# Two attentions of a two-layer network: the last projection of a step is rounded behind the next step's exponentials

## The reference

```python
q = (x @ Wq).reshape(b, n, HEADS, DIM_HEAD)
k = (context @ Wk).reshape(b, m, HEADS, DIM_HEAD)
v = (context @ Wv).reshape(b, m, HEADS, DIM_HEAD)
sim = einsum('bihd,bjhd->bhij', q, k) * SCALE
out = einsum('bhij,bjhd->bihd', softmax(sim), v) @ Wout + bout
```

## Time and profile before

| | us |
|---|---|
| median of 3 runs | 1023.07 |
| lowest, highest run | 1023.05, 1027.87 |
| the profiled execution's own time | 1026.1 |
| its span, first to last instruction | 1024.2 |
| attention A, first to last maximum | 61 to 459 |
| attention C, first exponential to last | 707 to 917 |

### The profile page before, as it was taken

One profiled execution on the slowest core, in us unless ns is written; L12 is line 12 of the kernel. 1 busy time (PEld: TensorE's weight loads), 2 busy tenths in 40 slices (PEclk: granted clock), 3 DMA queues, 4 the chain that ended last, 5 costly groups with the idle time before them and its releaser, 6 DMA issues. The chain is left out here.

```text
span 1024.2 us, 23424 instructions
## 1 busy us (share of the span) xinstructions
PE 824.4 (80%) x8736; PEld 506.2 (49%) x8808; DVE 756.2 (74%) x1541; ACT 709.8 (69%) x1179; POOL 627.7 (61%) x574
## 2 busy tenths in 40 slices
PE   3788799999999999997434999967777869875676
PEld 3534465556555656565122676622444536554243
DVE  3857888778877887775686455548979878876797
ACT  3269799889988999991441444436787877991574
POOL 1059677877787778780455666433686857872443
PEclk9989899999999999996666999989898999996799
DMA  8749999999999999993883988972999998990265
GB/s 212 235 80 159 173 178 185 173 167 180 178 184 170 178 172 168 175 178 62 204 292 70 182 187 181 165 243 47 185 169 192 234 203 134 189 171 16 39 116 134
DMA packets 504878, 167.96 MB, mean 164 GB/s; under 512 B 477728, under 2 KB 495328, under 8 KB 504736
## 3 DMA queue, kind: packets, MB, share of 16 engines
q1 hardware_dynamic: 501024, 156.25, 82.5%
q0 software_dynamic: 3744, 10.23, 3.5%
HBM read 37.04 MB, written 11.14 MB: 47 GB/s over the span
## 5 line engine op out<-in xcount | busy, mean ns | idle before, releaser
L521 POOL TENSOR_TENSOR A_PHL<-A_pr,A_PHL 128x508 f16<-128x508 f32 x256 | 294.0, 1154 | 92.1 <-ACT A_pr L802 91.7
L801 ACT ACTIVATE A_PHL<-A_ps,A_negmax 128x508 f16<-128x508 f32 x256 | 190.1, 743 | 14.5 <-DVE A_negmax L1051 12.8
L802 ACT ACTIVATE A_pr<-A_ps,A_negmax 128x508 f32<-128x508 f32 x256 | 191.8, 749 | 0.0
L521 POOL TENSOR_TENSOR C_PHL<-C_pr,C_PHL 128x512 f16<-128x512 f32 x128 | 149.7, 1177 | 58.0 <-ACT C_pr L802 57.8
L1051 DVE TENSOR_REDUCE A_negmax<-A_ps 128x2 f32<-128x1016 f32 x128 | 154.3, 1206 | 0.0
L647 PE MATMUL A_ps<-A_K,A_Q 64*128 64x512 f16 x768 | 106.5, 383 | 18.0 <-ACT A_pr L802 13.9
L665 PE MATMUL A_ps<-A_VH,A_PT 128*128 128x65 bf16 (+1 forms) x1024 | 108.1, 196 | 7.7 <-DMA A_PT<-A_PHL 7.7
L666 PE MATMUL A_ps<-A_VL,A_PT 128*128 128x64 f16 (+1 forms) x1024 | 108.1, 193 | 0.0
L667 PE MATMUL A_ps<-A_VH,A_PT 128*128 128x65 bf16 (+1 forms) x1024 | 108.0, 194 | 0.0
L665 PEld LDWEIGHTS A_ps<-A_VH,A_PT 128*128 128x128 f16 (+1 forms) x1024 | 94.8, 98 | 22.2 <-DMA A_PT<-A_PHL 10.7
L801 ACT ACTIVATE C_PHL<-C_ps,C_negmax 128x512 f16<-128x512 f32 x128 | 89.6, 700 | 20.2 <-DVE C_negmax L1051 17.8
(11 more groups left out here) (342 smaller groups left out, 2286.4 us busy)
## 6 DMA issues: line engine op xcount, KB each, us to landing
A_PT<-A_PHL SPq DMA_TRANSPOSE x256, 3.4
M_raw<-in_L_ffn_w_in SPq DMA_DIRECT2D x4, 1024.0 KB, 8.1
M_raw<-in_L_ffn_w_out SPq DMA_DIRECT2D x4, 1024.0 KB, 9.2
C_yc<-routed_rows SPq DMA_DIRECT2D x8, 512.0 KB, 5.1
M_rows<-M_xhl SPq DMA_DIRECT2D x4, 512.0 KB, 9.1
out<-X SPq DMA_DIRECT2D x16, 128.0 KB, 2.1
X<-in_x SPq DMA_DIRECT2D x1, 1536.0 KB, 14.0
ct_split<-A_CT SPq DMA_DIRECT2D x4, 384.0 KB, 3.0
```

The source lines that it names most:

```text
L521: pool.tensor_tensor(PHL[:, e % PRING, 1, 0:KEYS], pr[:, e % RING, 0:KEYS], PHL[:, e % PRING, 0, 0:KEYS], ALU.subtract).then_inc(pl_ready. ...
L801: a.activation(PHL[:, e % PRING, 0, 0:KEYS], o, ACT.Exp, bias=nm[:, n % 4, h:h + 1])
L802: a.activation(pr[:, e % RING, 0:KEYS], o, ACT.Exp, bias=nm[:, n % 4, h:h + 1]).then_inc(p_ready.sem, 1)
```

## The change

The jobs of each step are sorted so that q, k and v come last; this also is PE's order now. If the last job of a step is a q, k or v and the next step has fewer than two jobs, that job is late: ACT rounds it one step later, behind the next four exponentials (those of the step in which it was projected) instead of ahead of them, and DVE takes its low part behind the next maximum instead of ahead of it. All other jobs stay. In A 28 query, 25 key and 16 value jobs become late, in C 13 query and 13 key jobs. The sort puts a transpose or an image job ahead of a projection in 18 steps of A.

```diff
+    early, late_of = {}, {}
+    for step in sorted(at):
+        at[step].sort(key=lambda u: u[0] in "qkv")
+        spread = at[step][-1][0] in "qkv" and len(at.get(step + 1, [])) < 2
+        early[step] = at[step][:-1] if spread else at[step]
+        late_of[step] = at[step][-1:] if spread else []
...
             for g in range(G + TAIL):
                 if 1 <= g <= G:
                     weights(g - 1)
-                for u in at.get(g, []):
+                for u in late_of.get(g - 1, []) + early.get(g, []):
                     if u[0] in HI_KINDS:
                         high(u)
...
             for g in range(G + TAIL + 1):
-                for u in at.get(g - 1, []):
+                for u in early.get(g - 1, []):
                     low(u)
                 if g < G:
                     wait(v, s_filled, g + 1)
...
                     nb = g // U + 1
+                for u in late_of.get(g - 1, []):
+                    low(u)
+                if g < G:
                     if ipa and nb < B and g % U in (10, 12, 14):
```

## The result

The changed kernel takes 1055.63 us (median of 3, from 1055.27 to 1058.41) against 1023.07 before: ratio 1.0293, 95% interval 1.0245 to 1.0341. It is 32.6 us slower; 18 were forecast, and the time lies 0.6 us above the range. The profiled execution has a span of 1053.4 us, 29.2 more than that of before.

What follows compares the result with a forecast made beforehand. The prediction took PE to bound attention A. Added latency gave 15.7 us in A and 8.6 in C, 24.3 together, less 6 struck: +18 us, a median of 1041 us, range 1020 to 1055.

Steps and rivals of the forecast that it cites:

- late key, eleven pairs of A: Light key pairs of A shorter than 5.96 us grow to that floor from scores to scores; +4.2 us.
- late value, seven places: In A, value products one step after their projection wait for the late low part, 0.85 us at full cost; +4.6 us.
- normalised rows, steps 24, 56, 88: In A's batches 0 to 2, a late key's low part holds DVE ahead of the normalised rows; 1.5 us each, +4.5.
- layernorm chain, other pairs of steps 0 to 17: In A's batch 0, where DVE bounds, the maximum goes ahead of what PE waits for; 1.2 us twice, +2.4.
- C, six light quads (steps 12, 16, 28, 44, 48, 52): In C, query pairs shrink to 4.6 us, key pairs grow to 6.4; +0.5 per quad, +3.0 us.
- strike of a quarter: Over A and C, 6 us taken off the 24.3 because part falls where PE already waits for exponentials.
- the floor of 5.96: Shortest time in us from scores 4c-2 to scores 4c with a late key, through maximum, exponentials, rounding and low part.
- costs PE nothing by itself: Claim that putting the projection behind a transpose in 18 steps of A adds no PE time; 0 us.
- Works as meant: Rival: ACT's waits for projections in A and C are on the path, half recovered, 1010 us; chance 0.11.
- Cancel: Rival: boundaries find slack and C wins what A loses, 1019 to 1028 us; chance 0.11.
- The clock falls: Rival: every second of 24 new PE holes brings a stretch at the lower clock, +17 us, 1058; chance 0.06.
- what would show the forecast: Signs: some 30 PE waits of 0.7 to 1.1 us for keys; ACT waits for maximum instead; A batches 104 to 106 us.

Runs made afterwards that it cites:

- e7: The changed kernel with ACT rounding every job at its old place, only DVE's low parts late; ratio 1.0174 to the kernel before, A loop 410.4 us.
- e8: The changed kernel with DVE taking low parts at their old place, only ACT's roundings late; ratio 1.1329 to the kernel before, A loop 505.9 us.
- e3: The changed kernel, sorted as there, but only key jobs late; ratio 1.0210 to the kernel before.
- e4: The changed kernel, sorted as there, but only query jobs late; ratio 1.0021 to the kernel before.
- e1: The changed kernel with its sort alone and no job late; ratio 1.0066 to the kernel before.
- e2: The changed kernel with the image turn sorted last, so the values of steps 35, 67 and 99 aren't late; ratio 1.0227 to the kernel before.
- e9: The changed kernel without the sort and with only query jobs late; ratio 0.9972 to the kernel before.
- first and third set: Groups of experiments timed beside the kernel before, which had medians of 1024.8 us (first: e1 to e4) and 1026.5 us (third: e8 and two repeats of e9).

## Why the prediction was right, and where it wasn't

The direction and the mechanism hold: no work was added, latency was, in the loop score, maximum, exponential, rounding, low part, score. e7 and e8 take its two links apart, and e3 and e4 show that the distance to the first use is what counts. The size was too small, +18 for +32.6 us. The sizes of the terms, from the pitches of scores (the time from the scores of one pair of steps to those of the next) in both traces:

| term | forecast | measured |
|---|---|---|
| late key, eleven pairs of A | +4.2 | +6.1 |
| late value, seven places | +4.6 | +4.1 |
| normalised rows, steps 24, 56, 88 | +4.5 | -0.9 |
| layernorm chain, other pairs of steps 0 to 17 | +2.4 | -1.7 |
| image, steps 34, 66, 98 | 0 | +7.3 |
| steps 46 and 78 | 0 | +1.8 |
| pair of step 120, half clock | 0 | +1.7 |
| other pairs with `o` (22, 38, 54, 70, 86) | 0 | +1.4 |
| A (with 0.1 of other pairs) | +15.7 | +19.8 |
| C, six light quads (steps 12, 16, 28, 44, 48, 52) | +3.0 | +2.15 |
| C, all other pairs, the layernorm chains among them | +5.6 | +4.91 |
| C, last step | 0 | -0.62 |
| strike of a quarter | -6 | 0 |

That A came within 4.1 us of its forecast is in part luck. Two terms were 9.5 us too high (normalised rows, layernorm chain), and four that the forecast had at nothing or not at all (image, steps 46 and 78, step 120, `o`) brought 12.2.

**Late keys.** Ten of the eleven pairs sum to +4.7, for which the forecast has 3.9 (from the pitches before, the shortfalls of all eleven sum to 4.4, not 4.2); the floor of 5.96 is 5.98 at five places, 5.86 to 5.87 at three, and the pairs of steps 2 and 102 go beyond it, to 6.29 and 6.38. The eleventh, steps 118 and 119, lost 1.4 alone, where 0.3 was forecast: PE waits 2.21 us for the key. Timeline of ACT in the change:

```profile
446.93 0.68 ACT L807 ACTIVATE A_PHL<-A_ps,A_negmax 128x508 f16<-128x508 f32 x1 [0.82 <-DVE A_negmax L1057]
...
451.95 0.65 ACT L742 ACTIVATE A_K<-A_ps 128x512 f16<-128x512 f32 x1
```

The floor takes ACT as free when the maximum of step 118 is there. Here the exponentials of step 117 only begin at 446.93, 0.60 us after scores 118, and eight exponentials and the rounding of a transposed output (0.48) lie ahead of the key's: 5.02 us, then 1.43 to the scores, 7.05 in all.

**Late values.** The sizes hold at the steady places (0.82 to 0.84 us for 0.85). The parts of the term, 3.4, 0.4 and half of 0.85, add up to 4.2, not 4.6.

**Normalised rows.** The step that failed is "everything behind is 1.2 us later". It took the 2.38 us of the earlier trace rows as fixed, and moved them. The forecast itself named the collision with POOL further down and put it in the range, at plus or minus 1.0 each, where it belonged in this term: 1.0 gained, the rest of the delay covered.

**Layernorm in the first batch.** The chain costs nothing more: the pairs of steps 0, 4, 8 and 12 are 0.6 to 1.1 us shorter and that of step 10 longer by 1.1. A likely reason is that DVE is the bound there, so that a maximum that comes sooner is repaid; the prediction mentions those 0.6 us, and priced only the other side. No run separates this from chance: e1 and the kernel before have the same instructions there and differ by 2.3 us.

**Image.** The step that failed is that the order of PE "costs PE nothing by itself". It is true for PE's own work and false for what PE waits for: a job that is moved ahead of another is wanted earlier, and its producer, here a softmax on DVE, wasn't asked. e1 shows it by itself: 1.6 us from the sort alone (three pairs, 0.53 each). e2 splits the 7.3: 4.5 are there too (7.79 in place of 6.29 in each pair), since PE then waits for the late key's low part ahead of the image (5.4 us at three places, in the waits of e2), so these belong to the late key; the other 2.8, 1.2 of them half clock, go with the image's new place and the late value behind it.

**Steps 46 and 78.** Timeline of the change:

```profile
213.73 1.06 DVE L994 SCALAR_TENSOR_TENSOR ln_rstd<-ln_ve,ln_rstd 128x4 f32<-128x4 f32 x1
...
216.58 0.68 DVE L924 SCALAR_TENSOR_TENSOR A_K<-A_ps,A_K 128x512 f16<-128x512 f32 x1
...
217.31 0.82 PE L653 MATMUL A_ps<-A_K,A_Q 64*128 64x512 f16 x6 [0.81 <-DVE A_K L924]
```

This is the prediction's own mechanism (a chain, then a maximum, ahead of the low part) in a place it didn't look at, since PE had been the bound there: before, the low part ended 1.0 us ahead of the scores.

**The strike.** Next to the image's 7.3 it is the largest error on the total. "Part will fall where PE waits anyway" had no place of its own; 24.3 us without it stand against 19.8 + 6.4 = 26.2 in both loops. PE's waits for exponentials did go (13.9 to 3.6 us), and 5.1 of the 13.9 stood at steps where PE now waits for a key (4, 12, 24, 40, 56, 72, 88 and 120). But a term that is a floor less a pitch already holds the wait that stands in this pitch (0.82 us in the pair of step 118, say), so there the strike took it off twice.

**Outside the loops.** A begins 2.3 us sooner and the mixture, which no edit touches, is 4.4 us longer (247.7 to 252.1). In eight other profiled executions, that of before and those of the first and third set, it has 245.8 to 249.7 us at a mean granted clock of 0.81 to 0.83; in the change the clock is 0.79, and PE's busy time 185.0 us for 179.2 before. So the longest mixture is the one with the lowest clock; why the clock was lower stays open.

**The rivals.** "Works as meant" is right for one part: with late queries alone (e9) ACT's waits for queries in A shrink from 9.1 to 1.9 us, and the loops by 2 to 3 us in A (without the sort) and 2 to 8 in C. It fell with the keys and values. "Cancel" fell: C lost as well. "The clock falls" happened, but behind A's first batch in two places (steps 67 and 120), in C at one that had full clock before (step 20), and not in twelve. Of what would show the forecast, ACT's waits and their replacement came as said. The waits for a key are 31 (20 in A, 11 in C) for the 30 forecast, but 16 of A's 20 are 0.2 to 0.8 us instead of 0.7 to 1.1.

## What to carry to other kernels

Moving a step behind other work of its own engine is free only as far as its first consumer is away: count the steps from producer to first use (four for a query, two for a key, one for a value) and hold that against the latency that the move adds. If a list is sorted on the way, every job that comes sooner needs its own producer checked. Don't strike a share of a sum without a row that shows which waits cover which, and don't price parts one by one and add them: here 22.0 became 14.9.

Before an experiment, list which steps its edit reaches. A difference ahead of the first such step (2.3 us in e1) is the spread of the measurement, and an edit that reaches none (the sort in C) measures the same kernel again.

## What the runs showed of the hardware

**DVE beside POOL.** The same four instructions of 128x256 f32 took 2.38 us before, 2.93 in e7 and 1.37 in the change, by how much of them lay beside POOL's subtraction; and one on 128x4 numbers, 0.16 us in the median, took 1.06 at 213.73, where POOL has started at 213.63 (a subtraction lasts 1.15). In the kernel before, four such instructions of the chain ahead of step 16 took 1.01 to 1.12 us each (from 105.64 to 110.62), 3.6 us over four times 0.16, about as much as the 3.59 us that PE waits there. The Trainium skill, "SBUF — State Buffer", section "Who interferes with whom", states that the two share one port pair and lock each other out of it; this case's traces agree, with most of a subtraction's time paid even by an instruction of 0.16 us. The low parts that the change moved, with an input in PSUM, stayed at 0.68 to 0.69 us everywhere.

**The clock.** Behind holes of the same length PE went on at full or at half clock. The change has PE idle for 2.21 us ahead of step 120 and projects at the lower of the two levels behind it (a mean granted clock of 0.61 from 454.0 to 458.4):

```profile
453.38 0.82 PE L653 MATMUL A_ps<-A_K,A_Q 64*128 64x512 f16 x6 [2.21 <-DVE A_K L924]
454.14 1.07 PE L622 MATMUL A_ps<-ident,A_O 128*128 128x128 f32 x4
```

In e2 the same hole of 2.21 us stands at the same step, and the transpose behind it takes 0.66 (granted clock 1.00); that pair has 6.25 us there and 7.94 in the change. Likewise the image's hole of 2.28 us left the clock full at 172.56 and was followed by half clock at 279.65 (pairs of 8.33 and 9.53 us). In C a hole of 1.87 us was followed by half clock at step 20 (0.69 from 794.36 to 797.50; the pair grew from 5.29 to 6.04 us) and a hole of the same length by full clock at step 52 (1.00 from 901.9 to 905.0). So the price of one such hole in A was 0 or 1.2 to 1.7 us, near the 1.4 of the forecast, and no run shows which of the two comes.
